# The last batch's second graph layer in the banks of the scores, its mixes by rows, and cosine products of z itself

## What is computed

```python
def _L1_gnn_ref(h, causal_mask, Wl, Wg, Wv, Wo):
    z_l = h @ Wl
    z_g = h @ Wg
    v = h @ Wv
    A_l = _cosine_adjacency(z_l)      # max(zn @ zn.T, 0), zn = z / max(|z|, EPS), zero diagonal
    A_g = _rbf_adjacency(z_g, SIGMA_GRAV)   # exp(-d2 / 2), zero diagonal
    K_l = _row_stochastic_causal(A_l, causal_mask)   # A * mask / max(row sum, EPS)
    K_g = _row_stochastic_causal(A_g, causal_mask)
    K = w_l * K_l + w_g * K_g         # 0.9 and 0.1
    return jnp.einsum('bnm,bmd->bnd', K, v) @ Wo
...
h = jnp.maximum(_layernorm(x, axis=-1), 0.0)
x = x + _L0_gnn_ref(h, adj, ...)
h = jnp.maximum(_layernorm(x, axis=-1), 0.0)
x = x + _L1_gnn_ref(h, adj, L1_gnn_Wl, L1_gnn_Wg, L1_gnn_Wv, L1_gnn_Wo)
```

## Time and profile before

| | us |
|---|---|
| median of 3 runs (919.38 to 921.63) | 919.57 |
| the profiled execution | 919.7 |
| its span, first to last instruction | 917.9 |
| TensorE busy in the span | 835.4 (91%) |
| VectorE busy | 718.6 (78%) |
| ScalarE busy | 528.1 (58%) |
| GpSimd busy | 350.7 (38%) |

### The profile page before, as it was taken

How to read it: one execution, slowest core, us unless ns; L and a number is a source line. 1 busy time by engine, 2 the same in 40 slices (tenths; PEclk the granted TensorE clock), 3 DMA queues, 4 the chain that set the end, 5 groups by cost and what they waited for, 6 DMA issues and landing times.

```text
span 917.9 us, 15562 instructions
## 1 busy us (share of the span) xinstructions
PE 835.4 (91%) x4947; PEld 482.5 (53%) x4947; DVE 718.6 (78%) x2081; ACT 528.1 (58%) x1217; POOL 350.7 (38%) x416
## 2 busy tenths in 40 slices
PE   1479899999999999999999999999999999999976
PEld 0323345646464654646465554656465564646465
DVE  2777869788887979788797879888797978877435
ACT  1117585655647475665757575565758565575731
POOL 4424452443434253353525244353525334332310
PEclk9859999999999999999999999999999999999989
DMA  1322303031111203021120303021120303000000
GB/s 51 115 74 60 99 18 99 13 93 37 63 54 48 81 30 99 14 80 49 39 78 31 99 30 91 22 71 46 48 81 31 99 13 94 25 1 13 1 12 12
DMA packets 65536, 48.48 MB, mean 53 GB/s; under 512 B 10672, under 2 KB 65456, under 8 KB 65456
## 3 DMA queue, kind: packets, MB, share of 16 engines
q1 hardware_dynamic: 65456, 47.48, 17.2%
HBM read 30.28 MB, written 16.78 MB: 51 GB/s over the span
## 4 chain that ended last, share of the span: by engine, by line
PE 79%; DVE 11%; issue 4%; ACT 3%; POOL 1%; DMA 1%; SPq 1%; DVEq 0%; ACTq 0%; POOLq 0%
PE adj L578 12%; PE pv L571 12%; PE adj L583 12%; PE score L545 12%; PE turned L557 11%; PE turned L556 8%; PE work L589 5%; PE work L578 3%; DVE scrap L753 3%; PE work L653 2%; PE work L671 1%; DVE rbf_arg L785 1%; DVE zgT_parts L873 1%; DVE max_parts L761 1%; DVE zlT_parts L878 1%
## 5 line engine op out<-in xcount | busy, mean ns | idle before, releaser
L753 DVE CUSTOM_DVE_ANT_0 scrap<-score,mask_add 128x512 f32<-128x512 f32 x512 | 337.8, 684 | 45.3 <-PE score L545 41.4
L895 ACT ACTIVATE probs_t<-turned 128x512 f32<-128x512 f32 x512 | 293.5, 596 | 128.3 <-PE turned L557 125.9
L445 POOL TENSOR_TENSOR probs_t<-probs_t,keep_t 128x512 int32<-128x512 int32 x128 | 170.5, 1332 | 259.1 <-ACT probs_t L895 259.1
L545 PE MATMUL score<-qk_rows 96*128 96x512 bf16 x512 | 202.2, 397 | 12.3 <-DMA qk_rows<-split_dram 8.6
L557 PE MATMUL turned<-qk_rows 99*128 99x512 bf16 x512 | 195.7, 382 | 0.0
L556 PE MATMUL turned<-bar_t,ident_b 128*128 128x512 bf16 x384 | 147.1, 383 | 9.1 <-ACT probs_t L895 9.0
L571 PE MATMUL pv<-probs_t,v_cols 128*32 128x512 f32 x1024 | 136.4, 605 | 0.0
L545 PEld LDWEIGHTS score<-qk_rows 96*128 96x128 bf16 x512 | 50.0, 98 | 121.0 <-issue 74.1
L929 ACT ACTIVATE rbf_exp<-rbf_arg,rbf_bias 128x512 f32<-128x512 f32 x64 | 46.2, 722 | 63.1 <-DVE rbf_arg L785 63.1
L557 PEld LDWEIGHTS turned<-qk_rows 99*128 99x128 bf16 x512 | 50.6, 99 | 44.3 <-issue 1.2
L583 PEld LDWEIGHTS adj<-z,adj_cos 128*128 128x128 f32 x512 | 66.5, 190 | 11.2 <-DVE adj_cos L776 1.6
(11 more groups left out here) (114 smaller groups left out, 1198.3 us busy)
## 6 DMA issues: line engine op xcount, KB each, us to landing
qk_rows<-split_dram SPq DMA_DIRECT2D x384, 64.0 KB, 2.2
split_dram<-split SPq DMA_DIRECT2D x32, 384.0 KB, 2.4
x_sb<-in_x_dram SPq DMA_DIRECT2D x16, 256.0 KB, 2.9
out_dram<-out_sb SPq DMA_DIRECT2D x16, 256.0 KB, 2.3
qk_rows<-max_rows SPq DMA_DIRECT2D x96, 4.0 KB, 1.8
adj_sb<-in_adj_dram SPq DMA_DIRECT2D x1, 256.0 KB, 3.4
wqkv_sb<-in_L_gnn_W_qkv_dram SPq DMA_DIRECT2D x1, 192.0 KB, 2.7
bias_v<-in_L_gnn_b_qkv_dram SPq DMA_DIRECT2D x1, 64.0 KB, 2.9
```

Of the source, the lines that this page charges most:

```text
L445: pool.tensor_tensor(tile, tile, keep_t[:, w // HG % T, :], ALU.mult).then_inc(probs_masked.sem, 1)
L545: pe.matmul(score_bank[u % 2][:, :], qk_rows[0:ROWS, b % 2, 0, h, t * P:(t + 1) * P], qk_rows[0:ROWS, b % 2, 1, h, :], start=True, stop=Tr ...
L753: dve.tensor_tensor_reduce(scrap[:, u % 2, :], score_bank[u % 2][:, :], mask_add[:, u % T, :], -1.0, 3.0e38, ALU.add, ALU.min, neg_max[:, ...
L895: act.activation(probs_t[:, k % 4, w % HG, :], turned_bank[w % 2][:, :], ACT.Exp, scale=SCALE).then_inc(probs_ready.sem, 1)
```

## The change

Three things are changed.

*In every batch.* Cosine products take z_l as it is, so that `zlT` turns z and waits for z alone. The column norm goes into the values instead: v_cos = [vWo / norm, 1 / norm], with the weight 0.9 in the weights of vWo; the row norm cancels in the quotient, apart from the floor of the row sum, which becomes norm times EPS (`degree_floor`, one for each block). GpSimd's `z_norms` has six operations for four. Mixes have 129 columns for 130, z has a row of 385 words for 386. The squares have a buffer of their own, and the two products of z with h2T's high part no longer wait for its rest.

*In the last batch but one.* The mixes and outs stand later in the slots, the last of them behind the last batch's `h2T` (AT_BEFORE_LAST).

*In the last batch.* A table of its own (AT_LAST). z's four blocks go to the four banks of the scores, zlT to the PV bank, products 1 and 3 of each kind to the PV and work banks; VectorE takes the sums of squares; the mixes go through the adjacency row by row, all four blocks n for each row block m, into the four banks of the scores; the outs follow together, with one store for each block.

```diff
+AT_BEFORE_LAST = {
+    "mix_cos": (94, 95, 98, 99), "mix_rbf": (95, 97, 98, 104), "out": (96, 99, 101, 110), "store": (90,),
+}
...
+AT_LAST = {
+    "z": (72, 73, 77, 78), "z_copy": (67, 71, 72, 73), "z_sums": (72, 73, 78, 83), "z_norms": (81,),
...
+        def z_bank(batch, t):
+            return (score_bank + turned_bank)[t] if batch == B - 1 else adj_bank[t % 2]
...
+        def zl_bank(batch):
+            return pv_bank if batch == B - 1 else work_bank
...
+        def cos_bank(batch, m):
+            return pv_bank if batch == B - 1 and m % 2 else adj_bank[0]
...
+        def rbf_bank(batch, m):
+            return work_bank if batch == B - 1 and m % 2 else adj_bank[1]
...
+        def mix_bank(batch, n):
+            return (score_bank + turned_bank)[n] if batch == B - 1 else adj_bank[n % 2]
...
                     reached(pool, sums_ready, b)
-                    pool.tensor_scalar(norm_floor[:, :], square_sum[:, :, 0], LEAST_SQUARE, None,
-                                       ALU.max).then_inc(floor_ready.sem, 1)
                     reached(pool, rbf_exp_ready, b - 1)
                     reached(pool, col_filled, b - 1)
                     pool.tensor_scalar(rbf_bias[:, :], square_sum[:, :, 1], -0.5, None,
                                        ALU.mult).then_inc(rbf_bias_ready.sem, 1)
+                    pool.tensor_scalar(norm_floor[:, :], square_sum[:, :, 0], LEAST_SQUARE, None,
+                                       ALU.max).then_inc(floor_ready.sem, 1)
                     reached(pool, floor_ready, b)
-                    pool.tensor_tensor(inv_norm[:, :], norm_floor[:, :], minus_half[:, :],
+                    reached(pool, mix_filled, b - 1)
+                    pool.tensor_tensor(v_cos[:, :, D], norm_floor[:, :], minus_half[:, :],
                                        ALU.pow).then_inc(inv_norm_ready.sem, 1)
                     reached(pool, inv_norm_ready, b)
-                    reached(pool, zlT_filled, b - 1)
-                    pool.tensor_tensor(zl_unit[:, :, :], z[:, :, 0:D],
-                                       inv_norm[:, :].unsqueeze(2).broadcast_to([P, T, D]),
-                                       ALU.mult).then_inc(unit_ready.sem, 1)
+                    pool.tensor_tensor(v_cos[:, :, 0:D], z[:, :, 2 * D:3 * D],
+                                       v_cos[:, :, D:D + 1].broadcast_to([P, T, D]),
+                                       ALU.mult).then_inc(v_cos_ready.sem, 1)
+                    pool.tensor_tensor(norm[:, :], norm_floor[:, :], v_cos[:, :, D],
+                                       ALU.mult).then_inc(norm_ready.sem, 1)
+                    reached(pool, norm_ready, b)
+                    reached(pool, out_ready, b - 1)
+                    pool.tensor_scalar(degree_floor[:, :, 0], norm[:, :], KERNEL_EPS, None,
+                                       ALU.mult).then_inc(least_degree_ready.sem, 1)
...
+                    else:
+                        m = n
+                        reached(pe, z_ready, b)
+                        reached(pe, cos_ready, b, m + 1)
+                        for n in range(T):
+                            mix(cos_half(b, n), adj_cos, n, v_of_cos, [m])
...
-                    reached(pe, h2T_split, b)
-                    bank_free(pe, adj_turns[t % 2], b, "z", t)
...
+                    reached(pe, h2T_hi, b)
...
-                    reached(pe, unit_ready, b)
-                    bank_free(pe, work_turns, b, "zlT")
-                    turn_tiles(lambda t: zl_unit[:, t, :], zlT_filled)
+                    reached(pe, z_ready, b)
...
+                    turn_tiles(lambda t: z[:, t, 0:D], zlT_filled, zl_bank(b))
```

More of the change, by code:

```diff
@@ L85, in graph_blocks, with slots_of @@
     by_pool = [w for w in range(SLOTS) if w % HG not in MASK_BY_PE]
-    def due(slot, name):
[L89 to L93, removed]
+    def slots_of(name, batch):
+        table = {B - 1: AT_LAST, B - 2: AT_BEFORE_LAST}.get(batch, AT)
+        return [at + SLOTS * batch for at in table.get(name, AT[name])]
+    stages = {}
+    for name in AT:
+        for batch in range(B):
+            for nth, at in enumerate(slots_of(name, batch)):
+                assert (at, name) not in stages
+                stages[at, name] = batch, nth
+    def due(slot, name):
+        return stages.get((slot, name))
     def tile_due(slot, lag):
@@ L173, in graph_blocks @@
         norm_floor = sb("norm_floor", [P, T])
-        inv_norm = sb("inv_norm", [P, T])
+        norm = sb("norm", [P, T])
+        v_cos = sb("v_cos", [P, T, D + 1])
         rbf_bias = sb("rbf_bias", [P, T])
-        zl_unit = sb("zl_unit", [P, T, D])
         zlT_parts = sb("zlT_parts", [P, 2, N], F32R)
@@ L769, in _ @@
                                       ALU.subtract).then_inc(max_lo.sem, 1)
+                if (hit := due(s, "z_sums")) and hit[0] == B - 1:
+                    b, t = hit
+                    reached(dve, z_ready, b, t + 1)
+                    if t == 0:
+                        reached(dve, floor_ready, b - 1)
+                    for a in range(2):
+                        last = dve.tensor_tensor_reduce(z_square[:, t, a, :], z[:, t, a * D:(a + 1) * D],
+                                                        z[:, t, a * D:(a + 1) * D], 1.0, 0.0, ALU.mult, ALU.add,
+                                                        square_sum[:, t, a:a + 1])
+                    last.then_inc(sums_ready.sem, 1)
                 if hit := due(s, "cos_read"):
@@ L801, in _ @@
[L801 to L808 removed]
+                    blocks = [n] if b < B - 1 else range(T)
@@ new lines, in _ @@
+                    for n in blocks:
+                        reached(dve, mix_filled, b, n + 1)
+                        if n == 0:
+                            reached(dve, least_degree_ready, b)
+                        dve.tensor_tensor(degree[:, n, :], mix_bank(b, n)[:, D:D + 257:256], degree_floor[:, n, :],
+                                          ALU.max).then_inc(degree_ready.sem, 1)
+                    for n in blocks:
+                        reached(dve, degree_ready, b, n + 1)
+                        dve.reciprocal(inv_degree[:, n, :], degree[:, n, :]).then_inc(inv_degree_ready.sem, 1)
```

176 lines of the change are left out of this document (113 added, 63 removed).

## The result

The changed kernel takes **937.35 us** (median of 5 runs, 935.92 to 937.42) against 919.38 us (5 runs, 917.48 to 921.63): a ratio of 1.018, with a 95% interval of 1.0156 to 1.0205. It is slower by 1.8%, where 906.3 us and a range of 902 to 918.5 had been forecast. The profiled execution took 935.92 us, its span is 934.2.

A forecast was written before the change was run, and what follows sets the result against it. TensorE was taken to bound the full batches, a dependent chain the end. 919.7 - 10.8 (end) - 3.3 (full batches) + 1.2 (batches 13 and 14) - 0.5 (mixes) = 906.3 us; range 902 to 918.5.

The forecast's parts named there:

- What bounds the kernel: Full batches: TensorE busy 749.46 of 780 us; its largest wait, 13 times 1.4 us, set by GpSimd's order against VectorE.
- The sign of the full batches: Batches 0 to 12: VectorE's L761 starts before GpSimd's later mask, so TensorE's wait shrinks; -3.3 us (-6.5 to -1.3).
- 0.72 and 0.05: Chances of the forecast and of the rival that the end gains only half (-5.4 us, 911.7); together given as 0.76.
- The mask first: Rival, full batches: GpSimd's mask starts before VectorE's L761, TensorE's wait grows; +8.4 instead of -3.3 us, 918.0; chance 0.18.
- the end: Last batch's chain: earlier x1, faster z and products, gapless mixes, outs together; -10.8 us (8.5 to 13 earlier).
- full batches, wait: TensorE's wait for the maxima's turn in batches 0 to 12: 0.25 us less each, -3.3; the rival's +8.4.
- batches 13 and 14: Later mask delays batch 13's maxima turn by 0.5 us and batch 14's PV products by 0.65; together +1.2 (0.6 to 1.5).
- mixes of 129 columns: 1024 mix products one column narrower: 0.9 us saved if columns set the pace, 0 if weight loads do; taken -0.5.
- Batch 14's 0.65: Batch 14's PV products already wait for the mask (loads waited 0.42), so its 0.65 us delay goes through whole.
- the odd width: Rival, all 1024 mix products: odd rows of 385 and 129 words slow them; 964 if half as long again; chance 0.05.
- the forecast 7.3: Last batch, eight groups of three products and one column turn before the first mix: 6.3 to 10.9 us, taken 7.3.
- the mixes around h2T: Last batch: batch 14's mixes ahead of z give its products the full clock, 1.9 us in all (3.8 at lower level).

The follow-up runs named there:

- one operation more: Changed kernel with one more unused four-column operation on GpSimd, behind the degree floor and ahead of the mask: 904.01 us, ratio 0.982.
- the mask's wait: GpSimd's mask of tile 24 waits until VectorE has cut the next batch's maxima: changed kernel 892.17 us, kernel before 905.39 us.
- two operations more: Kernel before with two unused four-column operations on GpSimd, behind the unit-length rows and ahead of the mask: 935.32 us, ratio 1.018.
- the floor late: Changed kernel with GpSimd's norm and degree floor moved behind the mask and both cuts: 910.94 us, ratio 0.990.
- three more: Changed kernel with three more unused four-column operations on GpSimd, behind the degree floor and ahead of the mask: 891.15 us, ratio 0.968.

## Why the prediction was wrong

*What bounds the kernel: right.* The full batches are TensorE's, and their largest wait is set by who comes first at one place, GpSimd or VectorE. The rule of the Trainium skill named there ("SBUF — State Buffer", Who interferes with whom), that issue order decides who blocks, agrees with the rows shown: 1.26 us for a cut that came 0.05 behind the mask, 0.17 for one that came 0.04 ahead of it.

*The sign of the full batches: the step that failed.* The forecast put the mask's start at 397.19 to 397.32, against 397.23 for VectorE, and took VectorE as first. On the clock of the span before, the mask now starts at 397.17 (both spans are set equal at the rest of zgT, 394.67 and 405.83), 0.60 later than 396.57 and just below the bounds of 0.62 to 0.75. The sum was made of lengths put end to end. But the mask starts before the degree floor ends by its row: the floor runs from 408.13 to 408.36, the mask starts at 408.33. The rows of before show the same: L472 starts at 397.80, where the mask's 396.57 + 1.29 ends at 397.86. From start to start the part is 0.10 for the floor ahead of the power (the power starts 0.31 behind it, where it started 0.20 behind the row term) and 0.49 for the two new operations (from 407.84), 0.59, and the mask is first. The same place in the two traces, before:

```profile
393.94 0.24 POOL L501 TENSOR_SCALAR norm_floor<-square_sum 128x4 f32<-128x4 f32 x1 [0.90 <-ACT adj_cos L971]
394.26 0.23 POOL L505 TENSOR_SCALAR rbf_bias<-square_sum 128x4 f32<-128x4 f32 x1
394.46 1.04 POOL L508 TENSOR_TENSOR inv_norm<-norm_floor,minus_half 128x4 f32<-128x4 f32 x1
...
394.67 0.69 DVE L873 TENSOR_TENSOR zgT_parts<-work,zgT_parts 128x512 fp32r<-128x512 f32 x1 [1.32 <-ACT zgT_parts L977]
```

and after:

```profile
405.41 0.23 POOL L555 TENSOR_SCALAR norm_floor<-square_sum 128x4 f32<-128x4 f32 x1
405.72 1.04 POOL L559 TENSOR_TENSOR v_cos<-norm_floor,minus_half 128x4 f32<-128x4 f32 x1
...
405.83 0.69 DVE L993 TENSOR_TENSOR zgT_parts<-work,zgT_parts 128x512 fp32r<-128x512 f32 x1 [1.32 <-ACT zgT_parts L1096]
...
407.84 0.20 POOL L565 TENSOR_TENSOR norm<-norm_floor,v_cos 128x4 f32<-128x4 f32 x1
```

The trace of before held steps of this kind (its floor and row term start 0.32 apart, the power 0.20 behind). Put together from them (0.12 more for the floor, 0.32 and 0.20 for the new two) the mask would have come at 397.21, first by 0.02: an even race. It should not have been given 0.72 to 0.18 on what is called three quarters of a span of my own making (0.09 of 0.13, so 0.69). The chances also hold a slip: 0.72 and 0.05 are 0.77, not 0.76.

Where VectorE does come first, the forecast's sum is about right: with one operation more the first two cuts pass, the turn's wait is 1.00 where the forecast had about 1.1, and the kernel takes 904.01 us for 906.3.

*The price of the rival: mis-sized.* The mask first was listed as a rival, at 918.0. It happened, and cost 19.4 us more than that, the clock: the rival counted 0.64 for each batch, where 0.59 of wait and 1.64 of lower clock came together. The forecast weighed the clock at the end, where the trace of before shows the lower level, and nowhere else; it did not ask what a longer pause does to the work behind it, and so put that term at nothing. The upper end of the range hung on that. The trace of before had a longer pause of the same turn to look at, in the start: it waits 1.71 us, the clock is at 1.00 ahead of it (112 to 114 us) and at 0.50 behind it. In ten of the twelve profiles the clock falls behind that pause.

```profile
114.93 0.24 PE L633 MATMUL work<-ident_b,max_parts 128*48 128x128 bf16 x1 [1.71 <-DVE max_parts L768]
```

```profile
116.00:118.00 2.00, 1.71 (x5) 0.44 (x4) 1.54 (x6) 1.82 (x5) 1.69 (x5) 0.50 0.00 0
```

*The sum again, term by term, in us:*

| | forecast | rival's | measured |
|---|---|---|---|
| full batches, wait | -3.3 | +8.4 | +7.7 (13 x 0.59) |
| full batches, clock | none | none | +19.7 (12 x 1.64) |
| batches 13 and 14 | +1.2 | +1.2 | +0.6 |
| mixes of 129 columns | -0.5 | -0.5 | 0.0 |
| the end | -10.8 | -10.8 | -11.8 |

The measured ones add up to 16.2; the span grew by 16.3, from 917.9 to 934.2.

*Batches 13 and 14.* Batch 13's turn waits 0.70 where it waited 0.10, 0.6 more for the forecast 0.5, as the step said. Batch 14's 0.65 did not come: from the turn of batch 13 to y nothing changed (56.54 and 56.58). The row it rested on the earlier trace rows was misread. The PV loads at 860.20 need the masks up to tile 23, and the mask behind the norms is tile 24's; the next PV products that need it come 5 us later. In the trace after, the same loads wait as long, and the row names no releaser:

```profile
888.29 0.16 PEld L627 LDWEIGHTS pv<-probs_t,v_cols 128*32 128x32 f32 x8 [0.42 <-issue]
```

*Mixes of 129 columns.* One product takes 0.275 us by its row (median) for 130 and for 129 columns of the Gaussian's half, the next starts 0.112 behind it in both, and full stretches with the mask's wait take 50.79 us before and 50.83 after. A column less wins nothing, and the odd width, a rival of its own, costs nothing.

*The end: right in size and in nearly every link.* In us behind y:

| | x1 starts | z copied | first mix | mixes end | end of span |
|---|---|---|---|---|---|
| before | 3.8 | 16.4 | 33.7 | 41.7 | 45.6 |
| forecast | 2.5 | 12.8 | 22.2 | 29.5 | 34.8 |
| after | 2.7 | 13.1 | 21.3 | 28.6 | 33.8 |

The lower clock that the forecast allowed for in part of the products did not come (6.2 us for the forecast 7.3). One reason was wrong with the number right: the mixes around h2T don't hold z's clock, as their removal showed. Most of the gain lies between z's copy and the first mix, 17.3 us before and 8.2 after; how much of it the four banks, the new order and the clock each give, no run separates.

## What to carry to other kernels

Where one engine holds another, look for the pair of starts that are nearest to each other in the trace, and work out where a change puts them from start to start, not by adding lengths; if they end within a tenth of a microsecond, the sign is open, and it can be fixed by a wait instead of being left to chance. Price a longer pause of TensorE with the lower clock of the work behind it: here that was nearly three times what the pause had grown by. An engine that is mostly idle can be worth slowing down.

## What the runs showed of the hardware

A pause of TensorE in the same place, with the same work around it, was followed by a fall of the granted clock to 0.50 behind 12 of 13 pauses of 1.96 us (after), 7 of 13 of 1.74 (the kernel before with two operations more), and none of 13 of 1.49 (the floor late) or of 1.37 (before). Pauses of equal length went both ways within one execution, so what decides it is not the length alone; a fall cost 1.6 to 1.7 us each time.

VectorE's hold by GpSimd was decided by starts 0.02 to 0.06 us apart, with the same outcome in all thirteen batches of a run: a first cut 0.05 to 0.06 behind the mask took 1.26 us (after), a second one 0.04 ahead of it 0.17 to 0.18 (one operation more), a fourth one 0.02 ahead 0.17 to 0.18 (three more). Some of GpSimd's operations start 0.03 to 0.06 us before the one ahead ends by its row (the mask behind the degree floor, L522 behind the mask), others up to 0.09 behind it (the degree floor behind the norm, L524 behind L522).
